# Output matmuls spread over ten steps, max parts made ahead of an f16 turn and placed by two DMAs, a first pass 40 units ahead, row DMAs on two queues

## The reference

```
qk = (x @ Wqk.T + bqk) -> q, k per head;  v = x @ Wv.T + bv
attn = softmax(einsum('bhqd,bhkd->bhqk', q, k), axis=-1) / 8
x = layernorm(x + (attn @ v) @ Wo.T + bo)
Wg, Wu, Wd = dequant(q, s)        # groups of 128 inputs share a scale
x = layernorm(x + (silu(x @ Wg.T) * (x @ Wu.T)) @ Wd.T)
```

## Time and profile before

| | |
|---|---|
| median of 3 runs | 572.08 us (571.86, 572.08, 576.48) |
| the profiled execution | 576.28 us, span 574.5 us |
| PE, DVE, ACT, POOL busy | 531.3, 422.3, 406.5, 234.2 us |
| mean granted TensorE clock | 0.968 of 2.4 GHz |
| stretches of the profiled execution | start to about 62.8 us; steps to about 261 us; feed-forward to the end |

### The profile page before, as it was taken

How to read it: one execution, slowest core, us unless ns; L and a number is a source line. 1 busy time by engine, 2 the same in 40 slices (tenths; PEclk the granted TensorE clock), 3 DMA queues, 4 the chain that set the end, 5 groups by cost and what they waited for, 6 DMA issues and landing times.

```text
span 574.5 us, 7484 instructions
## 1 busy us (share of the span) xinstructions
PE 531.3 (92%) x2640; PEld 198.7 (35%) x2640; DVE 422.3 (74%) x725; ACT 406.5 (71%) x579; POOL 234.2 (41%) x267
## 2 busy tenths in 40 slices
PE   9897888989889989989999999999999999999992
PEld 3222212222122212214444445444454444544441
DVE  3589796978898799244877678766688667787666
ACT  1430675757677768997788877878878887787881
POOL 8020740002291255263546332673334733338442
PEclk9899597979999999999999999999999999999998
DMA  5593175002231003021004000010000010000101
GB/s 174 160 192 66 40 138 181 1 2 57 91 37 39 3 0 76 2 47 28 1 1 56 18 2 0 2 63 12 0 2 1 0 74 0 2 1 1 73 2 73
DMA packets 29237, 24.59 MB, mean 43 GB/s; under 512 B 19632, under 2 KB 21552, under 8 KB 29200
## 3 DMA queue, kind: packets, MB, share of 16 engines
q1 hardware_dynamic: 25328, 17.56, 11.4%
q0 software_dynamic: 3872, 6.56, 5.9%
HBM read 20.08 MB, written 4.19 MB: 42 GB/s over the span
## 4 chain that ended last, share of the span: by engine, by line
PE 72%; DVE 19%; ACT 3%; issue 2%; DMA 2%; SPq 1%; POOL 0%; POOLq 0%; ACTq 0%; DVEq 0%
PE ps L842 17%; PE ps L854 17%; PE ps L871 16%; DVE mxh L971 14%; PE ps L793 5%; PE ps L726 5%; PE ps L760 3%; PE ps L666 3%; PE ps L778 2%; PE ps L712 2%; ACT pbuf L557 1%; DMA stack<-mp 1%; SPq L335 1%; PE ps L880 1%; DVE st L1010 1%
## 5 line engine op out<-in xcount | busy, mean ns | idle before, releaser
L971 DVE TENSOR_REDUCE mxh<-ps 128x1 f32<-128x512 f32 x256 | 162.1, 682 | 28.4 <-PE ps L726 26.9
L1092 DVE TENSOR_SCALAR ps<-ps,ratio 128x512 f32<-128x512 f32 x168 | 121.8, 755 | 80.9 <-PE ps L854 80.5
L557 ACT ACTIVATE pbuf<-ps,gamma 128x1024 f32<-128x1024 f32 x128 | 135.2, 1115 | 49.7 <-PE ps L778 49.3
L612 ACT ACTIVATE ps<-ps,ratio 128x512 f32<-128x512 f32 x168 | 106.0, 657 | 41.7 <-PE ps L842 41.7
L871 PE MATMUL ps<-stack,wd 128*128 128x512 f16 x448 | 129.5, 379 | 0.6 <-POOL stack L484 0.6
L842 PE MATMUL ps<-arena,wg 128*128 128x512 f16 x448 | 115.3, 379 | 0.1
L854 PE MATMUL ps<-arena,wu 128*128 128x512 f16 x448 | 115.3, 379 | 0.0
L633 ACT ACTIVATE ps<-ps,ratio 128x512 f32<-128x512 f32 x156 | 102.7, 664 | 16.4 <-PE ps L871 16.4
L726 PE MATMUL ps<-stack 64*128 64x512 f16 x256 | 89.6, 407 | 13.6 <-DVE mxh L971 9.3
L482 POOL CAST stack<-pbuf 128x512 f16<-128x512 f32 x56 | 34.1, 609 | 141.3 <-DVE pbuf L1099 141.3
L793 PE MATMUL ps<-pbuf,arena 128*32 128x512 f32 x512 | 71.2, 629 | 0.6 <-ACT pbuf L557 0.6
(11 more groups left out here) (100 smaller groups left out, 330.5 us busy)
## 6 DMA issues: line engine op xcount, KB each, us to landing
arena<-xT SPq DMA_DIRECT2D x16, 256.0 KB, 5.6
x<-x SPq DMA_DIRECT2D x2, 2048.0 KB, 10.1
out<-x SPq DMA_DIRECT2D x3, 1024.0 KB, 4.2
wg<-gq POOLq DMA_DIRECT2D x4, 448.0 KB, 10.3
wu<-uq POOLq DMA_DIRECT2D x4, 448.0 KB, 12.7
wd<-dq POOLq DMA_DIRECT2D x2, 896.0 KB, 10.7
out<-x SPq DMA_DIRECT2D x4, 256.0 KB, 2.4
stack<-mp SPq DMA_DIRECT2D x48, 2.0 KB
```

The source lines that it names most:

```text
L557: nc.scalar.activation(pbuf[:, pi % 4, :].rearrange("p (a n) -> p a n", a=2), ps[:, 2 * (pi % 2):2 * (pi % 2) + 2, :], ACT.Exp, scale=gamm ...
L612: nc.scalar.activation(gbank[t % 2], gbank[t % 2], ACT.Copy, scale=gr[:, t % G, c:c + 1])\
L971: nc.vector.tensor_reduce(mxh[:, f % 2, qh, half:half + 1], ring_bank("first", n, 0), AX.X, ALU.max)\
L1092: nc.vector.tensor_scalar(ubank[t % 2], ubank[t % 2], ur[:, t % G, c:c + 1], None, ALU.mult)\
```

## The change

1. AHEAD is 40 units where it was 46, and two pieces of the placement of batch 0 stand before the first unit where three did; the others and the projections of batch 1 are issued after every second unit.
2. The maxima are split into three f16 parts right after `combine`, on 128x16 tiles in SBUF. The turn M then transposes all 48 columns in f16 with a new f16 identity, one DVE copy (`max_out`) brings the 48 rows to SBUF, and SP writes them by two DMAs of three partitions each. M stands one step later (step 6 and 14 of a block, not 5 and 13).
3. The 24 row DMAs of batch 1 are issued half by POOL and half by SP (`place_rows`); SP's stand ahead of `max_rows(1)`.
4. v of batch 1 is turned in bank 6, not 3, and step 0 waits for its banks and for batch 1's scales only; `place_v(1)` follows the units of step 0.
5. The wo stand at steps 4, 7, 10, 13 of a block, the statistics at 14 and 15, and block 2's layer norm and split move into feed-forward periods 5 to 8, block 3's to 9 to 14.

Before, the max rows were six DMAs each time, and the two rows L283 and L280 were not there. The diff:

```diff
--- before
+++ after
...
 FIRST = NB * NG * FG
-AHEAD = FG + 14
+AHEAD = FG + 8
 TILES = NB * G
...
         mx = sb("mx", [P, 2, HG * BT], F32)
-        mres = sb("mres", [HG * BT, P], F32)
-        mp = sb("mp", [HG * BT, 2, 3, P], F16)
+        mres = sb("mres", [P, HG * BT], F32)
+        mp = sb("mp", [P, 2, 3 * HG * BT], F16)
+        mrows = sb("mrows", [3 * HG * BT, 2, P], F16)
+        ident16 = sb("ident16", [P, P], F16)
         st = sb("st", [P, BT, 6], F32)
...
         AVB = 6
+        VTB = (3, AVB)
         gbank, ubank = (bank[4], bank[7]), (bank[5], bank[6])
...
             other = []
-            f, r = divmod(n + 3, KT)
+            f, r = divmod(n + 2, KT)
             if r == 0 and f < NB * NG:
...
-        WO_AT = (4, 6, 7, 8)
+        WO_AT = (4, 7, 10, 13)
         before = [("first", n, 0) for n in range(AHEAD)]
-        before.insert(FG + 5, ("M", 0, 0))
+        before.insert(FG + 2, ("M", 0, 0))
...
+        def place_rows(engine, jj):
+            for kind in range(2):
+                for part in range(2):
+                    for slot in range(4)[half_slots(kind, part)]:
+                        r, at = ROWS * jj + E * slot, kind * HD + jj * HD // 2
+                        src = (high, low)[part][at:at + HD // 2, :]
+                        if kind:
+                            engine.dma_start(ks[1][r:r + E, :, :], src).then_inc(s_stk1[jj], 16)
+                            continue
+                        for k in range(N // TB):
+                            engine.dma_start(qs[1][r:r + E, k, :, :], src[:, k * TB:(k + 1) * TB])\
+                                .then_inc(s_stk1[jj], 16)
...
                 u, g = divmod(f, NG)
-                sp.wait_ge(s_mrow, f + 1)
+                sp.wait_ge(s_rr["dve"], read_counts[ring_index["M", f, 0]])
...
                 b, k = divmod(u, N // TB)
-                for i in range(3):
-                    for jj in range(2):
-                        r = ROWS * jj + MROW + i
-                        sp.dma_start(qs[b][r:r + 1, k, 2 * g:2 * g + 2, :],
-                                     mp[2 * BT * jj:2 * BT * (jj + 1), f % 2, i, :]).then_inc(s_mld[g], 16)
+                for jj in range(2):
+                    r = ROWS * jj + MROW
+                    sp.dma_start(qs[b][r:r + 3, k, 2 * g:2 * g + 2, :],
+                                 mrows[6 * BT * jj:6 * BT * (jj + 1), f % 2, :]).then_inc(s_mld[g], 16)
...
+            sp.wait_ge(s_low, 3)
+            sp.wait_ge(s_fill, 6)
+            place_rows(sp, 1)
             max_rows(1)
...
-            sp.wait_ge(s_stk1, 16 * PARTS)
+            for jj in range(2):
+                sp.wait_ge(s_stk1[jj], 16 * PARTS)
             sp.wait_ge(s_vt, B)
...
             pool.wait_ge(s_low, 3)
-            for kind in range(2):
-                for part in range(2):
-                    for slot in range(4)[half_slots(kind, part)]:
-                        for jj in range(2):
...
+            place_rows(pool, 0)
             for g in range(0, G, G // 2):
...
                     inner_parts(p - 2)
-                if p == 5:
+                if 5 <= p < 5 + BT:
+                    x1_parts(NB - 2, p - 5)
+                if p == 10:
                     inverse(NB - 1)
-                if 7 <= p < 7 + BT:
-                    x1_parts(NB - 1, p - 7)
+                if 11 <= p < 11 + BT:
+                    x1_parts(NB - 1, p - 11)
                 for blk in range(NB - 1):
...
                     pe.wait_ge(s_projr, 3 * (b + 1))
-                    pe.wait_ge(s_unit, 3 * (b + 1))
+                    if b == 0:
+                        pe.wait_ge(s_unit, 3)
                     for t in range(BT):
-                        mm = nc.tensor.transpose(bank[3][:, t * P:(t + 1) * P], vtmp[:, t * P:(t + 1) * P], ident[:])
+                        mm = nc.tensor.transpose(bank[VTB[b]][:, t * P:(t + 1) * P], vtmp[:, t * P:(t + 1) * P], ident[:])
                     mm.then_inc(s_vt, 1)
...
-                    pe.wait_ge(s_mxc, u + 1)
-                    mm = nc.tensor.transpose(dst[0:HG * BT, 0:P], mx[:, u % 2, :], ident[:])
+                    pe.wait_ge(s_mrow, u + 1)
+                    mm = nc.tensor.transpose(dst[0:3 * HG * BT, :].bitcast(F16)[:, 0:P], mp[:, u % 2, :], ident16[:])
                 elif kind == "avT":
...
                 if kt == 0 and pair == 0:
-                    pe.wait_ge(s_mld[g], 16 * 6 * (u + 1))
+                    pe.wait_ge(s_mld[g], 16 * 2 * (u + 1))
                 if pi >= 2:
...
-                    pe.wait_ge(s_vc, 2 * B)
+                    pe.wait_ge(s_projr, 5)
+                else:
+                    pe.wait_ge(s_projr, 6)
+                    pe.wait_ge(s_unit, 6)
                 for j in range(2):
...
                 piece(p)
-            for n in range(3):
+            for n in range(2):
                 put(n)
-            later = [(put, n) for n in range(3, 6)] + [turn_v] + [(put, n) for n in range(6, len(placed))]
-            closely = len(later)
+            later = [(put, n) for n in range(2, 6)] + [turn_v] + [(put, n) for n in range(6, len(placed))]
             later += projections(1)
...
                 ring_use(*use)
-                if later and (n < closely or n % 2):
-                    piece(later.pop(0))
+                if n % 2:
+                    for _ in range(2 if len(later) > 15 else 1):
+                        piece(later.pop(0))
+            for p in later:
+                piece(p)
             for n in range(ALL):
...
-            def split_max(f):
+                part = [mp[:, f % 2, :].rearrange("p (j i q) -> p i j q", j=2, i=3)[:, i, :, :] for i in range(3)]
+                top = mx[:, f % 2, :].rearrange("p (j q) -> p j q", j=2)
+                rest = mres[:].rearrange("p (j q) -> p j q", j=2)
+                dve.wait_ge(s_mxc, f + 1)
+                nc.vector.tensor_copy(part[0], top).then_inc(s_msp, 1)
+                dve.wait_ge(s_msp, 3 * f + 1)
+                nc.vector.tensor_tensor(rest, top, part[0], ALU.subtract).then_inc(s_msp, 1)
+                dve.wait_ge(s_msp, 3 * f + 2)
+                nc.vector.tensor_copy(part[1], rest).then_inc(s_msp, 1)
+                dve.wait_ge(s_msp, 3 * f + 3)
+                nc.vector.tensor_tensor(part[2], rest, part[1], ALU.subtract).then_inc(s_mrow, 1)
+            def max_out(f):
...
                 if f >= 2:
-                    dve.wait_ge(s_mld[f % NG], 16 * 6 * (f // NG))
-                rows = ring_bank("M", f, 0)[0:HG * BT, 0:P]
-                nc.vector.tensor_copy(mp[:, f % 2, 0, :], rows).then_inc(s_msp, 1)
-                dve.wait_ge(s_msp, 2 * f + 1)
-                nc.vector.tensor_tensor(mres[:], rows, mp[:, f % 2, 0, :], ALU.subtract).then_inc(s_rr["dve"], 1)
-                wait_read(dve, "M", f, 0)
-                nc.vector.tensor_copy(mp[:, f % 2, 1, :], mres[:]).then_inc(s_msp, 1)
-                dve.wait_ge(s_msp, 2 * f + 2)
-                nc.vector.tensor_tensor(mp[:, f % 2, 2, :], mres[:], mp[:, f % 2, 1, :], ALU.subtract)\
-                  .then_inc(s_mrow, 1)
+                    dve.wait_ge(s_mld[f % NG], 16 * 2 * (f // NG))
+                nc.vector.tensor_copy(mrows[:, f % 2, :], ring_bank("M", f, 0)[0:3 * HG * BT, :].bitcast(F16)[:, 0:P])\
+                  .then_inc(s_rr["dve"], 1)
...
                     row_maxima(1)
-                if n == 38:
+                if n == AHEAD - 2:
                     scale_row(1)
-                if n == 43:
-                    place_scales(1)
-                if n == AHEAD - 1:
-                    place_v(1)
+            place_scales(1)
             for n in range(ALL):
...
                     ring_use(*use)
-                if n > STEPS and n % STEPS in (9, 10):
+                if n == 0:
+                    place_v(1)
+                if n > STEPS and n % STEPS >= 14:
                     for k in range(2):
-                        attention_stats(n // STEPS - 1, 2 * (n % STEPS - 9) + k)
-                if n > STEPS and n % STEPS == 10:
+                        attention_stats(n // STEPS - 1, 2 * (n % STEPS - 14) + k)
+                if n > STEPS and n % STEPS == 15:
                     mean_variance(n // STEPS - 1)
-                if n % STEPS == 12 and n > STEPS and apply_by_dve(n // STEPS - 1):
-                    apply(n // STEPS - 1)
                 if n == STEPS:
...
                         attention_stats(NB - 1, 2 * (p - 3) + k)
-                if p == 4:
+                if 5 <= p < 5 + BT:
+                    apply(NB - 2, [p - 5])
+                if p == 9:
                     mean_variance(NB - 1)
-                if 7 <= p < 7 + BT:
-                    apply(NB - 1, [p - 7])
+                if 11 <= p < 11 + BT:
+                    apply(NB - 1, [p - 11])
                 for blk in range(NB - 1):
```

25 lines of the change are left out of this document (10 added, 15 removed).

## The result

The changed kernel took **583.27 us** (median of 580.25, 580.81, 585.74 and 586.36), the kernel before 572.14 beside it: a ratio of 1.018, 95% interval 1.009 to 1.026. It is slower by 11 us, where I had forecast 569.0 and faster or no change; the time lies above my range of 563.0 to 574.5, at the price of rival (d), 583.7.

What follows compares the result with a forecast made beforehand. It took PE to bound the feed-forward and DVE's maxima the steps before it; -3.5 - 3.0 - 2.1 + 0.7 - 1.0 - 0.4 + 2.0 = -7.3 us from 576.28 gave 569.0 us, eight-in-ten range 563.0 to 574.5.

Steps and rivals of the forecast that it cites:

- (d): At every turn PE idles 1.95 us and the clock falls, seven turns losing 2.1 us each: 583.7 us; chance 0.08.
- The turn: At seven turns PE waits for DVE's four small operations, leaving DVE short of work: +0.1 us each, +0.7 together.
- (b): The two kinds of runs differ in places the change leaves alone, so the median run gives 564.8 us; chance 0.30.
- (a): Group 1's rows land slowly for their own reason (4.9 us); step 8's wait and clock fall stay: 574.1, chance 0.09.
- (c): SP, behind block 0's transposing DMAs, is late for the rows of group 5 or 7: 573.6 us; chance 0.07.
- The start: From the scale row to step 0: two units instead of five before the scales, step 0 earlier, -3.5 us.
- The wait at step 8: PE's wait for group 1's max rows, counted as 3.3 us, shrinks to 0.3: -3.0 us.
- The clock behind that wait: Steps 8 and 9 no longer run at the lower clock after the wait for rows: -2.1 us.
- The small wait for group 6's rows: A wait of 0.4 us for group 6's max rows, at 219.8 us in the chain, goes: -0.4 us.
- The output matmuls: Wo leaves step 24, where it met ACT's copy of av: 0.47 us for blocks 0 and 1, -1.0 us.
- What hides the rest: Norms moved into the feed-forward and SP's added row DMAs stay covered; without cover, eight times 0.7 us would show.
- The end of the units: Steps 52 to 55 lengthen and two wo move behind step 56: +2.0 us together.

Runs made afterwards that it cites:

- experiment 9: The kernel before with one edit: the load of wd issued behind block 0's additions, at about 150 us and not at 76; 569.01 us, ratio 0.990.
- experiment 5: The changed kernel with five matmuls of no use ahead of every turn's wait, written to the bank the turn overwrites; 576.31 us, ratio 1.002.
- 7: The changed kernel with POOL's load of wd moved behind the steps, x's load left behind the rows; one run, 578.72 us.
- experiment 6: The changed kernel with the load of x's first half moved on SP from behind group 1's max rows to behind group 2's; one run, 581.7 us.
- experiment 11: The changed kernel with 46 units ahead, old turn, old places of wo, statistics and norms, wd loaded behind block 0's additions, scale_ratios seven steps from the end; 561.74 us.

## Why the prediction was wrong

**The step that failed is "The turn".** I put it at +0.1 us each, for a shortage of units on DVE, and took the wait in which "PE does almost nothing" for harmless, since "two operations of PE lie within". The place and length of that stretch were right: I had it from 0.9 to 2.85 us behind the scores, and the trace has the scores at 73.86 and the next unit at 76.67, 2.8 us later. Both halves of its price were wrong. The step itself grew by 6.63 - 6.06 = 0.57 us, not 0.1: PE's order is fixed, so a turn that waits 1.27 us holds units, products with v and the next scores with it, and DVE has nothing to read meanwhile. And the clock fell. I put the point from which it falls between 1.9 and 2.5 us of idle because a wait of 1.85 had not lowered it and one of 2.48 had the earlier trace rows. The first of these is a misreading: the 1.85 us are idle time of ACT. PE's own wait there, in the kernel before, was 0.80 us:

```profile
156.49 0.39 PE L726 MATMUL ps<-stack 64*128 64x512 f16 x1 [0.80 <-DVE mxh L971]
```

So nothing in those rows spoke for a wait of 1.3 to 1.9 us as harmless, and the two of 1.95 and 1.71 us that PE had at 58.40 and 62.16 stood where the clock was 0.50. Nor was one case a ground for the other end: 2.48 us lowered it in the changed kernel and not in experiment 9, and 1.27 + 0.30 us lowered it behind some turns of an execution and not behind others. These traces show no length of a single wait that decides it; it is a chance, which seven turns take seven times, and it came four times in one trace and seven times in the next. Experiment 5 shows what it costs: the same steps, the wait filled, no fall behind a turn, and 583.3 us become 576.3.

**The rivals.** (d) was this mechanism, and its 583.7 us is the measured time; but that is partly luck: it counted 14.7 us of clock on top of my sum, where the runs have 7 of clock, 4.0 of longer steps and the rest in the points below. Its 0.08 was too low for the one thing that the change does at every turn. (b), that before's runs differ in clock at places the change leaves alone, is neither shown nor refuted: its runs follow the clock, but only one of them was traced, and experiment 9 has too few runs. My sum rests on that one, 4.2 us above the median. (a) came true in its landing, 5.8 us behind the second issue for the 4.9 it had, but not in its reason: without wd in flight the rows were in time. (c) came true only with six DMAs.

**The start** was right, by the way that I gave: -3.9 for -3.5, with DVE's scales at 55.80 us for 56.0.

**The wait at step 8**, -3.0 forecast: it went from 2.97 to 1.94 us. The rows were issued even earlier than I said (77.36; I had 79.0), and wd was issued 8.4 us earlier, but had not landed at 81: it took up to 16.5 us, not 13.0, to about 85. That wd delays the rows was right (7 against 6); that it would be gone in time was not, since I kept its duration. It may be SP's row DMAs, issued until 69.8 and now beside it, that slowed it; that is not shown. The load of x accounts for about 1 us (experiment 6). The rule that I weighed, from the Trainium skill, "DMA: Bandwidth & Descriptors", section "Queues, rings and completion order", has each DMA engine take turns between queues, packet by packet. Here the measurement decides against what I drew from it: rows on SP's queue landed in 5.6 to 5.8 us beside a load on POOL's, and in 1.70 without it.

**The clock behind that wait**, -2.1: steps 8 and 9 took 6.82 us, not 7.72: -0.9, with a clock of 0.57 from 84 to 88. The small wait for group 6's rows, -0.4, is gone; PE had waited 0.17 us there.

**The output matmuls**, -1.0: steps 20 to 35 took 51.68 us against 51.11, +0.57 where two turns alone make +1.14: so about -0.6 for a block, as forecast. But spreading them brought POOL's additions beside the turn: +1.0 us at 182.13 and at 235.72. "What hides the rest" did not look for that. The Trainium skill, "SBUF — State Buffer", section "SBUF: two separate sides", says that a DVE operation with two inputs in SBUF and a GpSimd operation that reads SBUF hold a shared pair of ports one after the other; the trace agrees, 1.16 us for 0.17, ended with POOL's operation.

**The end of the units**, +2.0: it came to +5.9. Steps 52 to 55 took 13.37 us in experiment 5, which lost no clock there, for 11.9 forecast and 10.42 before: of the 1.5 us missing, 1.0 is the port in the last turn's step (1.16 us for 0.17 there, too). The steps behind step 56 took 2.1 us longer, since the two wo there stretch three steps by 0.5 to 0.9 us each; I had 1.0. Step 56 gave 0.7 back. In the changed kernel's own trace steps 52 to 55 took 14.92 us: another 1.55 of clock, 0.50 from 238 to 241.

So experiment 5, at one clock 5 us above the kernel before, has in its steps: longer turns of groups 1 to 6 +3.4, the port +2.0, the rest of the end +3.4, the output matmuls -1.2, and up to step 6 -4.6. That makes +3.0. The other 2 us I cannot place: no execution of the kernel before at 0.981 was traced, and how long it waits at step 8 there is not known. Experiment 5 waits 3.06 us there, longer than the changed kernel's 1.94.

**What stays open**: why the clock falls behind one wait of 1.27 us and not behind the next of the same length, and by what way a load on one queue delays rows on another.

## What to carry to other kernels

Before moving work ahead of an operation in an engine's fixed order, count what that engine has left to do while it waits; if it is next to nothing, price both the wait and a clock that may fall behind it, at each repetition. Rank executions by granted clock before comparing their traces: here a low-clock execution of the one kernel stood beside the best of the other, and that hid two thirds of the loss. A spread that follows the clock points to waits of PE that are worth removing: experiment 11, which keeps the start of this change and takes away the waits at steps 8 and 17, is 2.2% faster than the kernel before, of which experiment 9 has 1.0% by moving one load. And see whose idle time a row gives: ACT's is not PE's.

## What the runs showed of the hardware

- Matmuls whose result is thrown away can be worth their time: five at each turn gave 7 us by the medians; ten runs with them spread over 1.6 us, four without them over 7.6.
- A PE wait of 2.48 us was followed by a clock of 0.57 in one execution (the changed kernel, 115 to 119 us) and of 1.00 in another (experiment 9), one of 1.28 us by 1.00 and by 0.50 (group 3 in the table of experiment 5).
- While the load of wd was in flight, small writes on another engine's queue landed 5.6 to 5.8 us after the second was issued, at 78 us and again at 151, for 1.70 without it (group 6 in the kernel before).
- A 128x16 operation of DVE with two inputs in SBUF took 1.16 us beside an addition of POOL, and 0.17 or 0.18 without one.
